# One block of a diffusion transformer on one core: ScalarE scales probabilities in two head pairs instead of four, and the five hand-written instruction lists and the bank table are dealt anew

## The chip, the cores and the metric

The kernel runs on one core of one Trainium2 chip. The metric is the device time in microseconds (us) of one launch. The kernel before takes 1402.81 us (median of 3 runs, 1401.66 to 1405.39). PE is TensorE, PEld its weight loads, DVE is VectorE, ACT ScalarE, POOL GpSimd and SP the engine that issues the loads and stores.

## The reference

32 batch elements, each 256 tokens of 128 features, go through one block: adaptive layer norm, causal attention with 16 heads of 64, and a feed-forward part that adds a gated MLP to a product-key expert lookup. Everything is float32.

```
h = layernorm(x) * (1 + ca) + sa
x = x + ga * attn(h)     # rmsnorm(h); q, k, v; softmax(q k^T * 64^-0.5, causal) v; sigmoid gates per head; Wout
h = layernorm(x) * (1 + cb) + sb
x = x + gb * ffn(h)
# ffn: silu(h Wg + bg) * (h Wu + bu) Wd + bd
#    + experts: sim = (h Wq) . keys, top 8 of 64 on both halves, their 8 best sums of 512,
#      softmax weights * silu(h . down_embed) into up_embed
```

## The kernel before, in words

One batch element is one turn (`body(i)`) of a software pipeline. Turn i runs the attention of batch i, the end of attention and the start of the FFN of batch i - 1, and the rest of the FFN of batch i - 2. Turns -1 and 0 have short lists of their own, turns 1 to 31 use the general list (3 to 30 of them in a hardware loop), and turn 32 has an own list again, which drains the pipeline. The change touches the general list, and two steps of turn 0.

Each engine has its own list of steps, written by hand: the calls at the end of `body` for POOL, ACT, DVE and PE. An engine works through its list strictly in that order, and each step begins with the semaphore waits it needs. So the order of the work is set by these lists alone; there is no planner.

The steps of attention go by pair of heads p = 0 to 7. On PE, `project_qk(p)` and `project_v(n)` (float32 split in a high and a low part, three matmuls each: the helper `mm3`, L1580 to L1582), then `scores(p)` (L1634, L1638), which works on halves of 64 rows of the array, `transpose_scores(p)` (L1648) and `weigh_values(p)` (L1661, L1665), which works on halves of 64 columns. All other work of PE uses the whole array of 128 x 128. Between them DVE takes the row maxima in place in PSUM (`row_max`, L1126), ACT the exponentials (`exp_scores`, L693), DVE the inverse and the coefficient (`invert` L1133, `coefficients` L1141) and the scaled probabilities (`normalise`, L1151). In the pairs listed in `SHARED`, DVE scales only head 0, and ACT scales head 1 with two activations (`scale_head`, L700). ACT copies the transposes to SBUF (`copy_transposes`, L685) and the outputs of `weigh_values` (L673).

Pairs take turns in two halves of the PSUM tensor pS. All other products of PE go through four PSUM banks, pW0 to pW3. The table `order` lists the 36 products of a turn; the n-th takes bank n mod 4, and has to wait until the product that stands before it in that bank is released by the engine that read it last. Thus the table decides who waits for whom: `("sim", 0)` is the first similarity product, `("hT", 0)` the transposed rows of the second layer norm, `("GU", c)` gate and up of the FFN, `("D", k)` the down products, `("ET", k)` the transposed expert weights, `("y", 0)` the FFN output.

Three chains matter below. `transpose_h` on PE writes hT; ACT modulates it (`modulate_h`, L793), makes its high part (`high_part`, L801), and DVE the low part (`low_part`, L1180), which releases it; only then can `similarity(0)` start. `gate_product(c)` (L1174) on DVE releases GU c. `shift(k)` (L1234) on DVE releases similarity k.

Of the kernel before, what the change touches and what calls it, by code (L numbers as in the profile page):

```python
# [43 lines left out]
SHARED = (1, 3, 5, 7)  # L44
# [3 lines left out]
def program(nc, x, norm_w, Wq, Wkv, Wout, Wgate, fWg, fbg, fWu, fbu, fWd, fbd, fWq, keys,  # L48
            down, up, cond, wmod, out):
    ctx = ExitStack()  # L50
    with ctx:
# [150 lines left out]
        def S(name):  # L202
# [33 lines left out]
        order = [("GU", 1, -2), ("D", 0, -2), ("V", 0, 0), ("PV", 6, -1), ("PV", 7, -1), ("V", 3, 0), ("QK", 2, 0),  # L236
# [232 lines left out]
        def _(pool):  # L469
# [24 lines left out]
            def body(i):  # L494
# [123 lines left out]
                candidates()  # L618
                products(1)
                rstd1()  # L620
                add_bias()
                weigh(0)
                add_heads(0)
                fold(0)
                rstd2()
                rms1()
                weigh(1)
                add_heads(1)
                fold(1)
# [4 lines left out]
        def _(act):  # L634
# [32 lines left out]
            def body(i):  # L667
# [150 lines left out]
                if isinstance(i, int) and i == 0:  # L818
# [16 lines left out]
                    scale_head(3)  # L835
# [22 lines left out]
                    scale_head(7)  # L858
# [48 lines left out]
                gate_up(1)  # L907
                down_tanh(0)
                copy_transposes(7, -1)
                values(0)  # L910
                exp_scores(0)
                weighted(6)
                values(3)
                weighted(7)
                queries(2)
                values(4)
                exp_scores(1)
                queries(3)
                queries(4)
                down_tanh(1)  # L920
                scale_head(1)
                copy_transposes(0, 0)
                copy_transposes(1, 0)
                queries(5)
                values(5)
                gate_up(2)
                exp_scores(2)
                exp_scores(3)
                total(0)
                values(1)  # L930
                gate_up(3)
                scale_head(3)
                queries(6)
                copy_transposes(2, 0)
                weighted(0)
                rows2()
                copy_transposes(3, 0)
                weighted(1)
                exp_scores(4)
                modulate_h()  # L940
                weighted(2)
                high_part(h2T_high, h2T, "hT")
                weighted(3)
# [7 lines left out]
                rms_scale()  # L951
                weighted(4)
                expert_exp(0)
                total(1)
                weighted(5)
                exp_scores(6)
                expert_exp(1)
                high_part(xT_high, xT, "xT")
                experts(1)
                exp_scores(7)  # L960
                scale_head(7)
                gate_up(0)
                copy_transposes(6, 0)
                queries(0)
                queries(1)
# [17 lines left out]
        def _(dve):  # L983
# [130 lines left out]
            def body(i):  # L1114
# [351 lines left out]
                bias_product(1)  # L1466
                ln1(aggregate1)
                gate_product(1)
                sum_top()
                gated_down(0)  # L1470
                row_max(0)
                invert_top()
                row_max(1)
                ln1(center1)
                choose(0, 0)
                choose(0, 1)
                invert(0)
                ln1(scale1)
                coefficients(0)
                invert(1)  # L1480
                normalise(0)
                coefficients(1)
                normalise(1)
                ln1(shift1)
                gated_down(1)
                choose(1, 0)
                row_max(2)
                row_max(3)
                invert(2)
                coefficients(2)  # L1490
                normalise(2)
                bias_product(2)
                invert(3)
                gate_product(2)
                gate_attention()
                add_residual()
                coefficients(3)
                stats2()
                aggregate2()
                ln1(square1)  # L1500
                normalise(3)
                bias_product(3)
                gate_product(3)
                choose(1, 1)
                row_max(4)
                row_max(5)
                invert(4)
                low_part(h2T_high, h2T, "hT")
                coefficients(4)
                normalise(4)  # L1510
                invert(5)
# [3 lines left out]
                row_largest(1)  # L1515
                shift(0)
                row_max(6)
                shift(1)
                invert(6)
                coefficients(6)  # L1520
                row_max(7)
                normalise(6)
                invert(7)
                coefficients(7)
                low_part(xT_high, xT, "xT")
                gate_output()
                finish()
                bias_product(0)
                gate_product(0)
                normalise(7)  # L1530
# [6 lines left out]
        def _(pe):  # L1537
# [49 lines left out]
            def body(i):  # L1587
# [268 lines left out]
                if isinstance(i, int) and i == B:  # L1856
# [55 lines left out]
                    late_project_up(1)  # L1912
                    return


                gate_up(1)
                project_down(0)
                transpose_scores(7, -1)
                project_v(0)
# [4 lines left out]
                project_v(3)  # L1924
                project_qk(2)
                project_v(4)
                project_qk(3)
                project_qk(4)
# [67 lines left out]
```

How the kernel before makes its waits and increments, by code:

```python
            def wait_free(self, name, k=0, after=(), off=None):  # L312
                job = self.apart(name, k, self.batch(name, k))
                if job:
                    for pn, pk in after:
                        self.wait_released(pn, pk, self.i + off)
                    full, free, n, count_n = job
                    if count_n > 1:
                        self.eng.wait_ge(free, count_n - 1)
                    elif (name, k, self.batch(name, k)) in drained:
                        pn, pk, turn = [j for m, j in enumerate(order) if m % NW == n and j[2] <= 0][-1]
                        self.wait_released(pn, pk, B - 1 + turn)
                    return
                need = {}
                prev = self.before(name, k)
                if prev and isinstance(self.i, int) and (prev[0], prev[1], self.i + prev[2]) in opened:
                    n = bank_of[name, k]
                    self.eng.wait_ge(open_free[n], n_opened[n])
                    if n == 0:
                        self.eng.wait_ge(su_act, 5)
                    prev = None
                for pn, pk, turn in [(*j, off) for j in after] + ([prev] if prev else []):
                    key = self.key(pn, pk)
                    need[key] = max(need.get(key, (turn, 0)), (turn, place[pn, pk] + 1))
                for key, (turn, n) in need.items():
                    self.eng.wait_ge(S(work_free[key]), self.nth(key, self.i + turn, n))
```

## Time and profile before

| | |
|---|---|
| median of 3 runs | 1402.81 us (1401.66 to 1405.39) |
| the profiled execution, its own time | 1400.69 us |
| its span, first to last instruction | 1398.8 us |
| PE busy / PEld busy | 1369.1 us (98%) / 1157.3 us (83%) |
| ACT / DVE / POOL busy | 1264.6 (90%) / 1214.9 (87%) / 1080.4 us (77%) |
| share of the chain that ended last | PE 93%, DVE 3%, ACT 2% |
| granted TensorE clock | 1.000 (2.4 GHz) |
| DMA | 27.74 MB, mean 20 GB/s |

The chain that ended last is followed back from the last instruction; 93% of it lies on PE. A turn of the loop is one period of a pattern that repeats 31 times. The ends of matmuls are modelled by the profiler, their starts are recorded: the difference of two starts is the reading to trust on PE. In the rows below, x4 on `scores` stands for two matmuls in two records each.

### The profile page before, as it was taken

How to read it: one execution, taken by the hardware profiler on the slowest of the kernel's cores; microseconds unless marked ns; L12 is line 12 of the kernel's file. 1: busy time of each engine (PE TensorE's matmuls, PEld its weight loads, DVE VectorE, ACT ScalarE, POOL GpSimd, SP SyncE). 2: the span in 40 equal slices, each digit the busy share in tenths (PEclk: the TensorE clock that was granted, in tenths of full speed). 3: DMA queues.
4: the chain of work that ended last, by engine and by line, in shares of the span. 5: the costliest groups of instructions: out<-in, count | busy, mean ns of one | idle time of the engine just before them, and what ended most of it. 6: DMA issues, size and time to landing. Idle time of an engine off the chain costs nothing.

```text
span 1398.8 us, 39734 instructions
## 1 busy us (share of the span) xinstructions
PE 1369.1 (98%) x11491; PEld 1157.3 (83%) x11491; DVE 1214.9 (87%) x5314; ACT 1264.6 (90%) x4212; POOL 1080.4 (77%) x1252
## 2 busy tenths in 40 slices
PE   6899999999999999999999999999999999999998
PEld 4778888888888888888888888888888888888877
DVE  6688898988898988898988898988898988898877
ACT  6889999999999999999999999999999999999975
POOL 2158888888888888888888888888888888888770
DMA  4000000000000000000000000000000000000000
GB/s 137 16 19 19 17 10 20 21 21 17 15 9 21 21 21 17 15 9 21 21 21 17 15 9 21 21 21 17 15 9 21 21 21 17 15 9 24 11 15 11
DMA packets 51042, 27.74 MB, mean 20 GB/s; under 512 B 10337, under 2 KB 50209, under 8 KB 51009
## 3 DMA queue, kind: packets, MB, share of 16 engines
q1 hardware_dynamic: 50768, 26.91, 7.3%
q10 hardware_dynamic: 240, 0.43, 0.1%
q8 instruction: 16, 0.26, 0.1%
q14 instruction: 18, 0.14, 0.0%
HBM read 23.02 MB, written 4.31 MB: 20 GB/s over the span
## 4 chain that ended last, share of the span: by engine, by line
PE 93%; DVE 3%; ACT 2%; issue 1%; POOL 1%; DMA 0%; SPq 0%; DVEq 0%; POOLq 0%
PE pW L1580 12%; PE pS L1648 12%; PE pW L1582 10%; PE pW L1581 10%; PE pW L1661 9%; PE pW L1689 8%; PE pS L1638 8%; PE pS L1634 7%; PE pW L1731 4%; PE pW L1734 4%; PE pW L1665 4%; PE pW L1722 2%; PE pW L1594 2%; ACT pS L693 1%; DVE pS L1126 0%
## 5 line engine op out<-in xcount | busy, mean ns | idle before, releaser
L693 ACT ACTIVATE pS<-pS,nmx 128x128 f32<-128x128 f32 (+1 forms) x1024 | 390.0, 437 | 31.3 <-DVE nmx L1126 30.7
L525 POOL TENSOR_TENSOR fexp<-fexp,fsum 128x512 f32<-128x512 f32 x240 | 316.5, 1347 | 90.6 <-DVE fexp L1277 90.6
L1126 DVE CUSTOM_DVE_ANT_0 pS<-pS,mask 128x128 f32<-128x128 f32 (+1 forms) x1024 | 332.3, 387 | 51.4 <-PE pS L1638 49.4
L516 POOL TENSOR_TENSOR fsum<-ex 128x512 f32<-128x512 f32 x248 | 251.8, 1047 | 1.3 <-ACT ex L741 1.3
L685 ACT COPY pT<-pS 128x768 f32<-128x768 f32 x256 | 206.1, 817 | 24.1 <-PE pS L1648 23.8
L1648 PE MATMUL pS<-ident,p_sb 128*128 128x128 f32 x1536 | 206.7, 274 | 6.8 <-DVE p_sb L1151 6.6
L1151 DVE TENSOR_TENSOR p_sb<-pS,coef 128x256 f32<-128x256 f32 (+2 forms) x512 | 208.9, 449 | 4.5
L693 ACT ACTIVATION_READ_ACCUMULATOR pS<-pS,nmx 128x1 f32 x1024 | 198.4, 194 | 0.0
L1648 PEld LDWEIGHTS pS<-ident,p_sb 128*128 128x128 f32 x1536 | 175.2, 141 | 27.6 <-DVE p_sb L1151 8.5
L1661 PE MATMUL pW<-pT,v 128*64 128x256 f32 x1024 | 162.3, 395 | 0.1
L1277 DVE TENSOR_SCALAR fexp<-fsum,top,rz 128x512 f32<-128x512 f32 x240 | 156.3, 702 | 0.0
L532 POOL TENSOR_TENSOR fexp<-fexp 128x512 f32<-128x512 f32 x120 | 152.4, 1291 | 4.7
L673 ACT COPY qk<-pW 128x512 f32<-128x512 f32 x256 | 154.6, 644 | 0.8 <-PE pW L1582 0.6
L1638 PE MATMUL pS<-qk 64*128 64x256 f32 x1024 | 155.1, 377 | 0.0
L1580 PE MATMUL pW<-xT_high,s_qkv_high 128*128 128x256 f32 x512 | 152.9, 299 | 1.3 <-DVE xT_low L1180 1.2
L1581 PE MATMUL pW<-xT_low,s_qkv_high 128*128 128x256 f32 x512 | 144.2, 282 | 0.0
L1582 PE MATMUL pW<-xT_high,s_qkv_low 128*128 128x256 f32 x512 | 143.9, 281 | 0.0
L1126 DVE DVE_READ_ACCUMULATOR2_ANT nmx<- 128x1 f32 x1024 | 141.5, 138 | 0.0
L1634 PE MATMUL pS<-qk 64*128 64x128 f32 x1024 | 120.7, 311 | 5.2 <-ACT pT L685 5.2
L1689 PEld LDWEIGHTS pW<-w_out,aoT 128*128 128x128 f32 x1024 | 116.8, 192 | 10.4 <-issue 10.3
L1689 PE MATMUL pW<-w_out,aoT 128*128 128x128 f32 x1024 | 122.7, 278 | 0.0
L1133 DVE RECIPROCAL pS<-pS 128x4 f32<-128x4 f32 x256 | 49.0, 192 | 82.3 <-ACT pS L693 82.2
(211 smaller groups left out, 3674.0 us busy)
## 6 DMA issues: line engine op xcount, KB each, us to landing
x_in<-in_L_attn_tokens SPq DMA_DIRECT2D x32, 128.0 KB, 2.1
x_res<-in_L_attn_tokens SPq DMA_DIRECT2D x32, 128.0 KB, 2.8
modB<-mods_dram SPq DMA_DIRECT2D x32, 128.0 KB, 2.9
modA<-mods_dram SPq DMA_DIRECT2D x31, 128.0 KB, 3.1
out<-yo SPq DMA_DIRECT2D x31, 128.0 KB, 1.9
modC<-mods_dram SPq DMA_DIRECT2D x32, 64.0 KB, 3.1
fsum<-in_L_attn_Wkv SPq DMA_DIRECT2D x1, 512.0 KB, 6.4
w_out<-in_L_attn_Wout SPq DMA_DIRECT2D x1, 512.0 KB, 7.3
```

The costliest lines, as they stand in the source:

```text
L516: ins = nc.gpsimd.tensor_tensor(fsum[:, k, h], ex[:, k, h, 0:NX].unsqueeze(2).broadcast_to([P, NX, NK]), ex[:, k, RH + h, :].unsqueeze(1). ...
L525: ins = nc.gpsimd.tensor_tensor(fexp[:, k, h, :], fexp[:, k, h, :], fsum[:, k, h].rearrange("p i j -> p (i j)"), ALU.mult)
L693: ins = nc.scalar.activation(ps, ps, ACT.Exp, bias=nmx[:, p % 2, h, k:k + 1], scale=-1.0, accum_out=den(p)[:, h, k:k + 1])
L1126: ins = nc.vector.tensor_tensor_reduce(out=ps, in0=ps, in1=mask[:, (1 - k) * P:2 * P], scale=-1.0, scalar=LARGEST, op0=ALU.add, op1=ALU.mi ...
L1580: mm(o, lhs[0], rhs[0], start=True, stop=False)
L1581: mm(o, lhs[0], rhs[1], start=False, stop=False)
L1582: return mm(o, lhs[1], rhs[0], start=False, stop=True)
L1634: mm(ps[:, h, 0:P], qk[r, p % 4, 0:P], qk[r, p % 4, N:N + P], start=True, stop=True, skip_group_check=True)
L1638: ins = mm(ps[:, h, P:SW], qk[r, p % 4, P:N], qk[r, p % 4, N:2 * N], start=False, stop=True, skip_group_check=True)
L1648: ins = tp(pS[:, p % 2, h, b * P:(b + 1) * P], p_sb[:, p % 2, h, b * P:(b + 1) * P], ident[:, :])
L1661: mm(bank[h * DH:(h + 1) * DH, 0:N], v[:, 0, hd], pT[:, p % 2, h, 0:2 * P], start=True, stop=False, skip_group_check=True)
L1689: ins = mm(w.bank("op")[:, k * D:(k + 1) * D], aoT[:, p, k * P:(k + 1) * P], w_out[:, p, :], start=p == 0, stop=p == NP - 1)
```

## The change

`SHARED` goes from pairs 1, 3, 5 and 7 to pairs 1 and 5: in pairs 3 and 7 DVE scales both heads, and the two `scale_head` steps of ACT go, in turn 0 too. The table `order` and the general lists of all four engines are written in another order. No other arithmetic is changed. The semaphore p1_ready counts two steps a turn instead of four.

```
-SHARED = (1, 3, 5, 7)
+SHARED = (1, 5)
...
-        order = [("GU", 1, -2), ("D", 0, -2), ("V", 0, 0), ("PV", 6, -1), ("PV", 7, -1), ("V", 3, 0), ("QK", 2, 0),
...
+        order = [("V", 3, 0), ("V", 0, 0), ("PV", 6, -1), ("PV", 7, -1), ("QK", 2, 0), ("V", 1, 0), ("QK", 3, 0),
+                 ("GU", 1, -2), ("GU", 2, -2), ("D", 0, -2), ("V", 4, 0), ("op", 0, -1), ("V", 5, 0), ("QK", 4, 0),
+                 ("PV", 0, 0), ("PV", 1, 0), ("D", 1, -2), ("QK", 5, 0), ("GU", 3, -2), ("PV", 2, 0), ("PV", 3, 0),
+                 ("hT", 0, -1), ("QK", 6, 0), ("QK", 7, 0), ("V", 2, 0), ("sim", 0, -1), ("ET", 0, -2),
+                 ("sim", 1, -1), ("PV", 4, 0), ("PV", 5, 0), ("y", 0, -2), ("ET", 1, -2), ("xT", 0, 1), ("QK", 0, 1),
+                 ("GU", 0, -1), ("QK", 1, 1)]
```

The general list of PE, new, with the old places of the steps left out:

```
+ transpose_scores(7, -1)  project_v(3)  project_v(0)  scores(0)  scores(1)  weigh_values(6)  weigh_values(7)
+ project_qk(2)  project_v(1)  project_qk(3)  gate_up(1)  transpose_scores(0, 0)  gate_up(2)  project_down(0)
+ transpose_scores(1, 0)  project_v(4)  scores(2)  scores(3)  project_out()  project_v(5)  project_qk(4)
+ weigh_values(0)  weigh_values(1)  project_down(1)  project_qk(5)  transpose_scores(2, 0)
+ transpose_scores(3, 0)  gate_up(3)  scores(4)  scores(5)  weigh_values(2)  weigh_values(3)  transpose_h()
+ project_qk(6)  project_qk(7)  project_v(2)  similarity(0)  transpose_experts(0)  transpose_scores(4, 0)
+ similarity(1)  transpose_scores(5, 0)  scores(6)  weigh_values(4)  weigh_values(5)  scores(7)
+ project_ffn(0)  transpose_experts(1)  transpose_x()  project_ffn(1)  transpose_scores(6, 0)  project_qk(0)
+ gate_up(0)  project_qk(1)
```

PE, the middle of a turn, before, from the transposes of pair 3 to `weigh_values` of pair 3 (pS<-qk is `scores`, pW<-pT,v is `weigh_values`, h is hT):

```order
L1648 MATMUL pS<-ident,p_sb 128x128 x6
L1634 MATMUL pS<-qk 128x128 x2
L1638 MATMUL pS<-qk 128x256 x2
L1661 MATMUL pW<-pT,v 64x256 x2
L1665 MATMUL pW<-pT,v 64x128 x2
L337 REGISTER_ALU
L1594 MATMUL pW<-ident,h 128x128 x2
L1634 MATMUL pS<-qk 128x128 x2
L1638 MATMUL pS<-qk 128x256 x2
L337 REGISTER_ALU
L1661 MATMUL pW<-pT,v 64x256 x2
L1665 MATMUL pW<-pT,v 64x128 x2
```

The same place now, with line numbers of the changed file:

```order
L1630 MATMUL pS<-qk 128x128 x2
L1634 MATMUL pS<-qk 128x256 x2
L364 REGISTER_ALU
L1630 MATMUL pS<-qk 128x128 x2
L1634 MATMUL pS<-qk 128x256 x2
L1657 MATMUL pW<-pT,v 64x256 x2
L1661 MATMUL pW<-pT,v 64x128 x2
L1657 MATMUL pW<-pT,v 64x256 x2
L1661 MATMUL pW<-pT,v 64x128 x2
L1590 MATMUL pW<-ident,h 128x128 x2
```

Scores 4 and 5 stand together, then `weigh_values` 2 and 3, and hT comes behind all four instead of between them.

DVE around the low part of hT, before: the maxima of pair 5, the inverse of pair 4, the low part, the coefficient and the probabilities of pair 4:

```order
L1126 ISA pS,nmx<-pS,mask 128x128
L1126 ISA nmx 128x1
L1126 ISA pS,nmx<-pS,mask 128x256
L1126 ISA nmx 128x1
L1133 RECIPROCAL pS<-pS 128x2x2
L1180 TENSOR_TENSOR h2T_low<-pW,h2T_high 128x256
L1141 SCALAR_TENSOR_TENSOR coef<-g_th,pS 128x4
L1151 TENSOR_TENSOR p_sb<-pS,coef 128x2x128
```

DVE there now, from the FFN products behind the maxima of pair 4 on (the four L1122 rows of `pS` are the maxima of pair 5):

```order
L1163 SCALAR_TENSOR_TENSOR pW<-pW,b_g,u_sb 128x256
L1170 SCALAR_TENSOR_TENSOR g_t<-g_t,pW 128x256
L1129 RECIPROCAL pS<-pS 128x2x2
L1137 SCALAR_TENSOR_TENSOR coef<-g_th,pS 128x4
L1117 REGISTER_ALU
L1122 ISA pS,nmx<-pS,mask 128x128
L1122 ISA nmx 128x1
L1122 ISA pS,nmx<-pS,mask 128x256
L1122 ISA nmx 128x1
L1122 ISA pS,nmx<-pS,mask 128x128
L1122 ISA nmx 128x1
L1122 ISA pS,nmx<-pS,mask 128x256
```

The inverse and the coefficient of pair 4 moved ahead of the maxima of pair 5; the low part of hT stands right behind those maxima as before, but now these follow the inverse.

## Rows read from the trace of the kernel before

**Rows 1.** The page, its first line.

```profile
span 1398.8 us, 39734 instructions
```

**Rows 2.** Chain in order of time: start, length, what; output projection of two bodies.

```profile
609.87 3.77 PE pW L1689 x32
...
651.83 3.77 PE pW L1689 x32
```

**Rows 3.** Busy us (x instructions): PE, PEld, DVE, ACT, POOL; clock; DMA share; GB/s.

```profile
426.00:468.00 42.00, 42.00 (x356) 35.62 (x355) 37.31 (x165) 38.95 (x131) 35.05 (x41) 1.00 0.06 17
```

**Rows 4.** Timeline of PE: start, length (us), instruction; scores 2, 3, output projection.

```profile
608.29 0.49 PE L1634 MATMUL pS<-qk 64*128 64x128 f32 x4
608.61 0.60 PE L1638 MATMUL pS<-qk 64*128 64x256 f32 x4
609.05 0.39 PE L1634 MATMUL pS<-qk 64*128 64x128 f32 x4
609.27 0.60 PE L1638 MATMUL pS<-qk 64*128 64x256 f32 x4
609.80 3.84 PE L1689 MATMUL pW<-w_out,aoT 128*128 128x128 f32 x32
```

**Rows 5.** Timeline of PE, where `project_v(1)` ends and gate/up 3 begins.

```profile
614.07 0.28 PE L1582 MATMUL pW<-xT_high,s_qkv_low 128*128 128x256 f32 x1
614.35 0.38 PE L1580 MATMUL pW<-h2T_high,s_g_high 128*128 128x256 f32 x1
614.57 0.28 PE L1581 MATMUL pW<-h2T_low,s_g_high 128*128 128x256 f32 x1
614.69 0.28 PE L1582 MATMUL pW<-h2T_high,s_g_low 128*128 128x256 f32 x1
```

**Rows 6.** Timeline of DVE: three instructions that free a bank.

```profile
613.88 0.42 DVE L1174 SCALAR_TENSOR_TENSOR g_t<-g_t,pW 128x256 f32<-128x256 f32 x1
...
622.65 0.42 DVE L1180 TENSOR_TENSOR h2T_low<-pW,h2T_high 128x256 fp32r<-128x256 f32 x1
...
629.27 0.68 DVE L1234 TENSOR_TENSOR sh<-pW,top_s 128x512 f32<-128x512 f32 x1
```

**Rows 7.** Timeline of PE, FFN output: first half, then second half.

```profile
630.01 1.15 PE L1731 MATMUL pW<-w_d,g_t 128*128 128x128 f32 x8
631.00 1.06 PE L1734 MATMUL pW<-w_up,eT 128*128 128x128 f32 x8
...
633.04 1.05 PE L1731 MATMUL pW<-w_d,g_t 128*128 128x128 f32 x8
633.93 1.06 PE L1734 MATMUL pW<-w_up,eT 128*128 128x128 f32 x8
```

**Rows 8.** Timeline of PE: scores 4, and the first transposes of the experts.

```profile
618.17 0.49 PE L1634 MATMUL pS<-qk 64*128 64x128 f32 x4
...
622.67 0.60 PE L1722 MATMUL pW<-ident,d_t 128*128 128x128 f32 x4
```

**Rows 9.** Timeline of DVE: row maxima of pair 4; pair 6 inverted, maxima of 7.

```profile
619.25 0.30 DVE L1126 CUSTOM_DVE_ANT_0 pS<-pS,mask 128x128 f32<-128x128 f32 x1 [0.48 <-PE pS L1638]
...
631.63 0.19 DVE L1133 RECIPROCAL pS<-pS 128x4 f32<-128x4 f32 x1 [1.68 <-ACT pS L693]
...
632.06 0.30 DVE L1126 CUSTOM_DVE_ANT_0 pS<-pS,mask 128x128 f32<-128x128 f32 x1
...
633.29 1.01 DVE L1151 TENSOR_TENSOR p_sb<-pS,coef 128x256 f32<-128x256 f32 x2
```

**Rows 10.** Timeline of ACT: first and last record of the exponentials of pair 4.

```profile
620.02 0.34 ACT L693 ACTIVATE pS<-pS,nmx 128x128 f32<-128x128 f32 x1
...
621.40 0.19 ACT L693 ACTIVATION_READ_ACCUMULATOR pS<-pS,nmx 128x1 f32 x1
```

**Rows 11.** Groups by shape, 400 to 1240 us: probabilities scaled by DVE.

```profile
L1151 DVE TENSOR_TENSOR p_sb<-pS,coef 128x512 f32<-128x512 f32 x80 | 54.3, 678 | 0.0
...
L1151 DVE TENSOR_TENSOR p_sb<-pS,coef 128x128 f32<-128x128 f32 x80 | 23.0, 287 | 1.4
```

More of the change, by code:

```diff
@@ L834, in body @@
                     queries(4)
-                    scale_head(3)
                     copy_transposes(2, 0)
@@ L1465, in body @@
                 ln1(stats1)
-                bias_product(1)
+                row_max(0)
+                row_max(1)
+                invert(0)
+                sum_top()
+                coefficients(0)
                 ln1(aggregate1)
[L1468 to L1471, printed above, removed]
+                normalise(0)
                 invert_top()
-                row_max(1)
                 ln1(center1)
+                invert(1)
+                coefficients(1)
+                normalise(1)
                 choose(0, 0)
                 choose(0, 1)
-                invert(0)
+                bias_product(1)
+                gate_product(1)
                 ln1(scale1)
[L1479 to L1486, printed above, removed]
                 row_max(2)
+                bias_product(2)
+                gate_product(2)
                 row_max(3)
+                gated_down(0)
+                gate_attention()
                 invert(2)
+                add_residual()
                 coefficients(2)
-                normalise(2)
-                bias_product(2)
                 invert(3)
-                gate_product(2)
-                gate_attention()
-                add_residual()
                 coefficients(3)
                 stats2()
+                normalise(2)
                 aggregate2()
-                ln1(square1)
                 normalise(3)
+                choose(1, 0)
+                choose(1, 1)
+                gated_down(1)
+                row_max(4)
                 bias_product(3)
                 gate_product(3)
-                choose(1, 1)
-                row_max(4)
+                invert(4)
+                coefficients(4)
                 row_max(5)
-                invert(4)
                 low_part(h2T_high, h2T, "hT")
-                coefficients(4)
                 normalise(4)
+                ln1(shift1)
                 invert(5)
@@ L1913, in body @@
                     return
-                gate_up(1)
-                project_down(0)
                 transpose_scores(7, -1)
+                project_v(3)
                 project_v(0)
@@ L1923, in body @@
                 weigh_values(7)
[L1924 removed]
                 project_qk(2)
[L1926 to L1935 removed]
+                project_v(1)
+                project_qk(3)
+                gate_up(1)
+                transpose_scores(0, 0)
+                gate_up(2)
+                project_down(0)
+                transpose_scores(1, 0)
+                project_v(4)
                 scores(2)
@@ L1938, in body @@
                 project_out()
-                project_qk(6)
-                gate_up(3)
-                transpose_scores(2, 0)
+                project_v(5)
+                project_qk(4)
                 weigh_values(0)
                 weigh_values(1)
+                project_down(1)
+                project_qk(5)
+                transpose_scores(2, 0)
                 transpose_scores(3, 0)
+                gate_up(3)
                 scores(4)
+                scores(5)
                 weigh_values(2)
+                weigh_values(3)
                 transpose_h()
-                scores(5)
-                weigh_values(3)
+                project_qk(6)
                 project_qk(7)
-                transpose_experts(0)
                 project_v(2)
                 similarity(0)
+                transpose_experts(0)
                 transpose_scores(4, 0)
@@ L1967, in body @@
                 project_qk(0)
+                gate_up(0)
                 project_qk(1)
```

80 lines of the change are left out of this document (35 added, 45 removed), and 5 rows, old and new, of the table order.

## The prediction, written before the changed kernel had run

> **What bounds the kernel now.** I read four views, in this order. The page first: the span is 1398.8 us [rows 1], and the profiled execution took 1400.69 us, 1.9 us around the span and 2.1 us under the median of 1402.81. The chain of waits in order of time second: it lies on PE, and the output projection of one turn starts at 609.87, that of the next at 651.83 [rows 2]. So a turn lasts 41.96 us, and the general list is run 31 times: 1301 of the 1399 us. Third the windows: in 42.00 us of the loop PE is busy for 42.00, DVE for 37.31, ACT for 38.95, POOL for 35.05, at the full clock [rows 3]. Nobody else is full. Last the timeline of PE, read by starts, since a full PE can still lose time in two ways that "busy" hides: by changing the shape in which it works, and by short waits that the modelled ends of matmuls cover. Both are there.
>
> Changes of shape. Scores work on halves of 64 rows, `weigh_values` (PV below) on halves of 64 columns, all else on the whole array; V n is `project_v(n)`. Two scores that follow each other start 609.05 - 608.61 = 0.44 apart (second part of the first to first part of the next), and a score and the output projection behind it 609.80 - 609.27 = 0.53: 0.09 for leaving the shape. The first scores after other work need 608.61 - 608.29 = 0.32 for their first part, the second 609.27 - 609.05 = 0.22: another 0.10 in the new shape [rows 4]. A change thus costs up to 0.19 us, and at least the 0.09 of leaving.
>
> Short waits. At 614.07 the last matmul of V 1 starts, at 614.35 the first of gate/up 3, at 614.57 its second, at 614.69 its third [rows 5]. The usual step is 0.12, so that the two steps of 0.50 hold 0.26 of waiting: the bank is released by gate_product, which ends at 613.88 + 0.42 = 614.30, 0.05 before PE starts [rows 6]. The same pattern stands three times more in a turn, each behind DVE. The FFN output starts at 630.01, 0.06 behind the end of shift(1) (629.27 + 0.68) [rows 6, 7]; its first half takes 631.00 - 630.01 = 0.99 to the next line, the second half, which waits for nobody, 633.93 - 633.04 = 0.89 [rows 7]: 0.10 lost. The low part of hT (622.65 + 0.42) ends just so before V 2, and the low part of xT before QK 0. I take 0.12 for each of these two, near the 0.10. In all 0.26 + 0.10 + 2 x 0.12 = 0.60 us a turn.
>
> The Trainium skill, "TensorEngine Tiling (Array Packing)", section Key Properties, says that changing the tiling mode drains TensorE, while changing the tile alone does not. Read so, a change between rows and columns would cost as much as one from the whole array, and the sum would be 3 x 0.19 instead of the 0.45 below. The rows here bear the direction out.
>
> **The change part by part.**
>
> Changes of shape go. Before, hT stood between two small groups: whole, scores 4, PV 2, hT, scores 5, PV 3, whole: six changes. Now it is whole, scores 4 and 5, PV 2 and 3, hT: three. In the rest of the list I count eleven before and eleven now (scores 0,1 and PV 6,7: three; scores 2,3: two; PV 0,1: two; scores 6, PV 4,5, scores 7: four). So 17 become 14. Three times 0.09 to 0.19 is 0.27 to 0.57; I take 0.15 each, nearer the scores rows, where both parts were seen: -0.45 us a turn.
>
> The four short waits go. In the new table gate/up 3 has PV 0 before it in its bank, which ACT copies out; V 2 has PV 3; the FFN output has the transposed experts; shift(1) and gate_product are no longer awaited there. QK 0 still needs the low part of xT, now 2.7 us behind xT (second half of the FFN output, transposes of pair 6), but DVE has it directly behind pair 6's probabilities. -0.60 us a turn; each may leave a rest, so 0.40 to 0.60.
>
> A new short wait comes. Similarity 0 needs the low part of hT, and DVE has put the inverse, the coefficient and the maxima of pair 5 in a row ahead of it. From the start of scores 4 the chain is: 1.08 to the first maxima (619.25 - 618.17) [rows 8, 9]; 0.77 to ACT's first exponential (620.02 - 619.25); 1.57 to the end of the last (621.40 + 0.19) [rows 10], and 0.03 to DVE; 0.43 from an inverse through the coefficient to the next maxima (632.06 - 631.63); 1.23 for these (633.29 - 632.06) [rows 9]; 0.42 for the low part, 0.06 to PE [rows 6, 7]. Sum 5.59 us. PE's way to similarity 0 in the same stretch: before, scores 4 to the first transposed experts took 622.67 - 618.17 = 4.50 [rows 8] and held scores 4 and 5, PV 2 and 3, hT and QK 7. Now QK 6 joins (6 steps of 0.12 = 0.71) and V 2 (3 steps of 384 columns, 0.18 each by their width, = 0.53); three shape changes leave, here at nearly their full price, 0.55: 5.19 us. PE arrives 0.40 early and waits: +0.40. From below, 0.2 if ACT and DVE hand over earlier than in these rows (the maxima may begin as soon as the scores end); from above 0.7, because the transposes of pair 5, scores 6 and PV 4 and 5 stand close behind on the same chain, and may each add a tenth.
>
> DVE and ACT. In pairs 3 and 7 DVE now scales both heads. Its shapes are 678 ns for 128x512 in place of 287 ns for 128x128, the 128x256 being in both [rows 11]: +0.39 us, twice a turn. DVE goes to 38.1 us of a turn of 41.3, and is still not full. ACT loses two pairs of activations. In the loop both are hidden by PE's list: transposes of pair 7 now have pair 6's transposes, QK 0, gate/up 0 and QK 1 before them, 2.8 us behind the FFN output, where DVE needs its 0.42 + 0.42 + 0.43 and 1.0 for pair 7, some 2.3. If that cover is gone, each tenth costs 3 us. In turn 0 there is little PE work to hide behind, and pairs 3 and 7 come 0.4 us later each: +0.8 us, between 0 and 2.
>
> The moved steps of POOL (bias, inverse roots, folds) cost nothing: POOL has 7 us free in 42, and its weighing of the experts is needed half a turn later. The loads on SP wait for the same releases and have turns to spare at 17 GB/s [rows 3]. Bounds for both: 0 to 2 us in all.
>
> Sum: 31 x (-0.45 - 0.60 + 0.40) = -20.2, and +0.8: -19.4 us. On the profiled execution 1400.69 - 19.4 = 1381.3; on the median shown 1402.81 - 19.4 = **1383 us**. Own range: -0.85 to -0.42 a turn, 1377 to 1391.
>
> **The rivals.**
>
> A: no new wait. The maxima of pair 5 run early enough and similarity 0 finds its operand. For it: DVE idled for 0.48 us before the maxima at 619.25 [rows 9], so it has room. Against it: the idle time ends in a wait for PE, the chain above is latency, and room does not shorten it. 31 x 1.05 = 32.6, less 0.8: 1371 us.
>
> B: no change. A PE that is busy 42.00 of 42.00 has nothing to give, the pipeline evens out the steps of 0.1 us. Against it the release times of rows 6, which stand right ahead of the late starts. 1403 us, within 3. The Trainium skill, "Perfetto Trace Analysis", section Identifying the Most-Contended Engine, warns that matmul busy is no measure of closeness to the limit and names the share of weight loads; that is 35.62 of 42.00 here, which speaks against this rival too.
>
> C: slower, through pair 7. Its probabilities are now wholly on DVE and stand behind gate_output and finish, which wait for the FFN output; its transposes open the next turn of PE. The slack worked out above is 0.5 us. It decides the sign once DVE is 0.5 + 0.65 = 1.15 us later than its rows say, for instance if the inverse of pair 7 finds ACT late with its exponentials. At 1.6 us late: 31 x 0.45 = +14, and 0.8: 1418 us. Against it: the idle times of DVE, 1.68 us before one inverse alone [rows 9].
>
> D: half the gain. The wait of similarity 0 is 0.7 and the followers on its chain take another tenth or two: 31 x 0.2 = 6, less 0.8: 1398 down to 1391 us.
>
> **How the numbers follow.** Forecast 0.63, A 0.15, D 0.13, B 0.05, C 0.04. The range is 1371 to 1395: it takes in A and most of D. About 0.3% (4 us) is what a measurement of this kernel tells from no change. Faster holds the forecast, A and most of D: 0.90; within 0.3% B and a rest of D: 0.06; slower 0.04.
>
> **What would show it.** The chain in order of time should have output projections about 41.3 us apart. In the PE timeline scores 5 should start 0.76 behind scores 4, gate/up 3 and V 2 should step by 0.12 and 0.18 from their predecessors, and the first similarity matmul should start 0.06 behind the end of L1176 on DVE, with some 0.4 us more than a step before it. A turn of 40.9 would show rival A, one of 41.96 rival B; a wait of the transposes of pair 7 for p_sb in the loop would show C. My sum would be wrong if the price of a shape change is paid again somewhere else, or if a wait that I have not placed stands in the second half of the turn.

## The result: slower, against the prediction

The changed kernel takes 1416.57 us (median of 3, 1415.22 to 1417.55) against 1402.81 before: ratio 1.0076, 95% interval 1.0056 to 1.0096, so 0.8% slower. Predicted was 1383. The profiled execution took 1417.55 us, its span is 1415.8.

### The profile page after: what moved, and what is told of

The parts are those of the page before. It is cut to its first block, busy times and chain, and to the rows that moved or that the text cites. A ratio compares the mean times of both kernels' runs of the same rounds, so it can differ in the third digit from the quotient of the medians.

```text
span 1415.8 us, 40018 instructions
## 1 busy us (share of the span) xinstructions
PE 1366.0 (96%) x11491; PEld 1161.4 (82%) x11491; DVE 1253.4 (89%) x5314; ACT 1230.7 (87%) x4084; POOL 1069.6 (76%) x1252
## 4 chain that ended last, share of the span: by engine, by line
PE 39%; POOL 20%; DVE 15%; issue 14%; ACT 11%; DMA 0%; ACTq 0%; SPq 0%; POOLq 0%; DVEq 0%
POOL fexp L525 10%; PE pS L1644 6%; POOL fexp L532 5%; DVE pS L1122 5%; PE pS L1634 4%; PE pW L1727 4%; PE pW L1730 4%; ACT pS L693 4%; PE pS L1630 4%; PE pW L1576 3%; PE pW L1657 3%; PE pW L1577 3%; PE pW L1578 3%; POOL wsum L535 3%; DVE h L1031 2%
## 5 line engine op out<-in xcount | busy, mean ns | idle before, releaser
L693 ACT ACTIVATE pS<-pS,nmx 128x128 f32<-128x128 f32 (+1 forms) x1024 | 397.1, 456 | 59.0 <-DVE nmx L1122 58.8
L525 POOL TENSOR_TENSOR fexp<-fexp,fsum 128x512 f32<-128x512 f32 x240 | 304.1, 1299 | 107.1 <-DVE fexp L1273 107.1
L1122 DVE CUSTOM_DVE_ANT_0 pS<-pS,mask 128x128 f32<-128x128 f32 (+1 forms) x1024 | 333.0, 390 | 56.6 <-PE pS L1634 55.2
L1147 DVE TENSOR_TENSOR p_sb<-pS,coef 128x256 f32<-128x256 f32 (+2 forms) x512 | 233.4, 498 | 4.6
L693 ACT ACTIVATION_READ_ACCUMULATOR pS<-pS,nmx 128x1 f32 x1024 | 216.7, 212 | 0.0
L673 ACT COPY qk<-pW 128x512 f32<-128x512 f32 x256 | 172.7, 675 | 16.2 <-PE pW L1578 15.9
L532 POOL TENSOR_TENSOR fexp<-fexp 128x512 f32<-128x512 f32 x120 | 156.7, 1326 | 4.7
L1122 DVE DVE_READ_ACCUMULATOR2_ANT nmx<- 128x1 f32 x1024 | 144.8, 141 | 0.0
L1630 PEld LDWEIGHTS pS<-qk 64*128 64x128 f32 x1024 | 82.8, 185 | 43.7 <-issue 25.9
L1273 DVE TENSOR_SCALAR fexp<-fsum,top,rz 128x512 f32<-128x512 f32 x240 | 115.0, 544 | 0.0
```

The source lines that it names most:

```text
L525: ins = nc.gpsimd.tensor_tensor(fexp[:, k, h, :], fexp[:, k, h, :], fsum[:, k, h].rearrange("p i j -> p (i j)"), ALU.mult)
L532: ins = nc.gpsimd.tensor_tensor(fexp[:, k, h, :], fexp[:, k, h, :], fexp[:, k, h + 1, :], ALU.add)
L693: ins = nc.scalar.activation(ps, ps, ACT.Exp, bias=nmx[:, p % 2, h, k:k + 1], scale=-1.0, accum_out=den(p)[:, h, k:k + 1])
L1122: ins = nc.vector.tensor_tensor_reduce(out=ps, in0=ps, in1=mask[:, (1 - k) * P:2 * P], scale=-1.0, scalar=LARGEST, op0=ALU.add, op1=ALU.mi ...
L1147: ins = nc.vector.tensor_tensor(o, pS[:, p % 2, mine, cols_of(k)], coef[:, p % 2, mine, k:k + 1].broadcast_to(o.shape), ALU.mult)
L1630: mm(ps[:, h, 0:P], qk[r, p % 4, 0:P], qk[r, p % 4, N:N + P], start=True, stop=True, skip_group_check=True)
```

## The profile after

The page of the changed kernel: the span answers to [rows 1], the second line is the busy time of each engine, the last the shares of the chain that ended last ("issue" is time in which an engine waited for nothing that the profile shows).

```profile
span 1415.8 us, 40018 instructions
...
PE 1366.0 (96%) x11491; PEld 1161.4 (82%) x11491; DVE 1253.4 (89%) x5314; ACT 1230.7 (87%) x4084; POOL 1069.6 (76%) x1252
...
PE 39%; POOL 20%; DVE 15%; issue 14%; ACT 11%; DMA 0%; ACTq 0%; SPq 0%; POOLq 0%; DVEq 0%
```

PE is still busy for 96%, but it is no longer the chain: 39%, where [rows 2] lay on PE from turn to turn. The window of one turn, with the columns of [rows 3]:

```profile
594.00:636.30 42.30, 41.74 (x356) 35.58 (x354) 38.50 (x165) 37.88 (x127) 34.52 (x40) 1.00 0.06 17
```

PE now leaves half a microsecond of a turn open, and DVE has gone from 37.31 to 38.50 us.

Where the 17.0 us between the two spans stand is read from the first scores of a turn. I counted from turn 3 to turn 31, 28 turns, and what lies ahead and behind (starts on PE in us; the last column is the span less the second):

| kernel | scores 0 of turn 3 | of turn 31 | mean turn | behind it |
|---|---|---|---|---|
| before | 135.75 | 1311.37 | 41.99 | 87.43 |
| changed | 138.50 | 1325.95 | 42.41 | 89.82 |

The loop lost 11.8 us, the start 2.75, the end 2.4. The forecast was a turn of 41.31.

In the loop both executions ran at a granted clock of 1.00. Outside it they did not: in the changed kernel's execution the clock fell to its lower level, 1.2 GHz, for 3.4 us three times, at 33.7, 91.7 and 1368.3 us, and in that of before never. The same stretch in both (columns as above), changed kernel first:

```profile
33.70:37.10 3.40, 3.40 (x18) 2.65 (x14) 1.37 (x8) 0.80 (x1) 0.00 (x0) 0.50 0.00 0
```

```profile
33.70:37.10 3.40, 3.40 (x34) 2.62 (x34) 1.37 (x8) 1.89 (x6) 0.00 (x0) 1.00 0.00 0
```

PE issued 18 matmuls in place of 34. From 20 to 30 us it had been busy for 7.74 us, before for 7.72, so its own work doesn't tell the two executions apart. Part of what the start and the end lost is therefore the clock and not the change.

The steps on PE can be checked one by one. Timeline of PE in the changed kernel, start and length in us (scores 4 and 5; end of V 2 and similarity 0; end of similarity 1 and transposes of pair 5; first half of the FFN output):

```profile
625.91 0.49 PE L1630 MATMUL pS<-qk 64*128 64x128 f32 x4
...
626.65 0.46 PE L1630 MATMUL pS<-qk 64*128 64x128 f32 x4
...
631.08 0.34 PE L1578 MATMUL pW<-s_qkv_high,xT_low 128*128 128x384 f32 x1
631.68 0.47 PE L1576 MATMUL pW<-s_sim_high,h2T_high 128*128 128x512 f32 x1 [0.27 <-DVE h2T_low L1176]
...
634.03 0.39 PE L1578 MATMUL pW<-s_sim_high,h2T_low 128*128 128x512 f32 x1
634.71 0.87 PE L1644 MATMUL pS<-ident,p_sb 128*128 128x128 f32 x6 [0.29 <-ACT p_sb L700]
...
638.80 1.16 PE L1727 MATMUL pW<-w_d,g_t 128*128 128x128 f32 x8
639.80 1.06 PE L1730 MATMUL pW<-w_up,eT 128*128 128x128 f32 x8
```

Scores 5 stand 0.74 behind scores 4 (0.76 predicted). Similarity 0 starts 0.60 behind the last matmul of V 2, whose step is 0.18: a wait of 0.42, predicted 0.40. The transposes of pair 5 were predicted to follow their predecessor; a step of similarity is 0.23, here it is 0.68: a wait of 0.45, in other turns up to 0.77 (0.58 in the mean), that no step of mine had. It is behind DVE, by way of ScalarE, which scales head 1 of pair 5. The chain of the same turn in order of time (start, length, what):

```profile
631.26 0.28 DVE h2T_low L1176
631.54 0.93 DVE p_sb L1147 x2
632.47 1.12 DVE h L1031
...
633.73 0.17 DVE coef L1137
...
634.19 0.48 ACT p_sb L700
...
634.71 0.87 PE pS L1644 x6
```

`ln1(shift1)` (h <- h, modA) now stands between the probabilities of pair 4 and the inverse of pair 5, and takes 1.12 us of the chain. Groups by shape from 400 to 1240 us, before and after: count, busy us, mean ns.

```profile
L1277 DVE TENSOR_SCALAR fexp<-fsum,top,rz 128x512 f32<-128x512 f32 x160 | 104.5, 704 | 0.0
L1035 DVE TENSOR_TENSOR h<-h,modA 128x256 f32<-128x256 f32 x20 | 10.6, 532 | 0.0
L1041 DVE CUSTOM_DVE_ANT_0 sq<-h 128x128 f32<-128x128 f32 x40 | 10.1, 289 | 0.0
L1026 DVE TENSOR_TENSOR h<-h,modA 128x256 f32<-128x256 f32 x20 | 8.1, 404 | 0.0
```

```profile
L1273 DVE TENSOR_SCALAR fexp<-fsum,top,rz 128x512 f32<-128x512 f32 x160 | 76.7, 544 | 0.0
L1031 DVE TENSOR_TENSOR h<-h,modA 128x256 f32<-128x256 f32 x20 | 26.1, 1305 | 0.0
L1037 DVE CUSTOM_DVE_ANT_0 sq<-h 128x128 f32<-128x128 f32 x40 | 18.4, 494 | 0.0
L1022 DVE TENSOR_TENSOR h<-h,modA 128x256 f32<-128x256 f32 x20 | 17.2, 859 | 0.0
```

The same four operations on the same data: shift1 went from 532 to 1305 ns, scale1 from 404 to 859, square1 from 289 to 494, and `choose` down from 704 to 544. The operations with an input in PSUM kept their lengths within 0.02 us. What changed for these four is what POOL does meanwhile. Timeline of DVE and of POOL in the changed kernel, two turns:

```profile
632.38 1.21 DVE L1031 TENSOR_TENSOR h<-h,modA 128x256 f32<-128x256 f32 x1
...
674.69 1.51 DVE L1031 TENSOR_TENSOR h<-h,modA 128x256 f32<-128x256 f32 x1
```

```profile
632.04 1.28 POOL L532 TENSOR_TENSOR fexp<-fexp 128x512 f32<-128x512 f32 x1
...
674.65 1.27 POOL L532 TENSOR_TENSOR fexp<-fexp 128x512 f32<-128x512 f32 x1
```

POOL's instruction ends at 632.04 + 1.28 = 633.32, shift1 at 632.38 + 1.21 = 633.59. In the other turn POOL ends at 675.92, shift1 at 676.20. Shift1 ends 0.27 or 0.28 behind the end of the POOL instruction in flight, whenever it started. It isn't slowed, it is held. The trace of before, which I had, says so already (DVE, then POOL):

```profile
606.20 0.55 DVE L1035 TENSOR_TENSOR h<-h,modA 128x256 f32<-128x256 f32 x1
...
607.27 2.32 DVE L1277 TENSOR_SCALAR fexp<-fsum,top,rz 128x512 f32<-128x512 f32 x2
```

```profile
605.17 1.29 POOL L525 TENSOR_TENSOR fexp<-fexp,fsum 128x512 f32<-128x512 f32 x1
...
607.86 1.45 POOL L525 TENSOR_TENSOR fexp<-fexp,fsum 128x512 f32<-128x512 f32 x1
```

POOL ends at 606.46, shift1 at 606.75; it had started so late in POOL's instruction that it lost a tenth. The two `choose` end at 607.27 + 2.32 = 609.59, which is 0.28 behind POOL's 609.31. Elsewhere a `choose` takes 0.54.

The Trainium skill, "SBUF — State Buffer", section Who interferes with whom, states this: VectorE and GpSimd share one pair of ports as an exclusive lock; a VectorE instruction with two SBUF inputs contends with a GpSimd instruction that reads SBUF, so does one in a 2-port mode, and "Whoever issues first gets the shared pair for the whole instruction". The trace agrees: two inputs (shift1, scale1, square1) are held and so is `choose` with one, those with an input in PSUM aren't, and POOL's instructions that start behind a held one read 1.45 to 1.47 us in place of 1.28. No row here shows in which mode `choose` runs. The prediction didn't weigh this rule.

## Experiments

Three theories. **L, lock**: three operations of layer norm 1 (scale1, shift1, square1) were moved to places where POOL's long instructions run, and the wait stands on the way to the transposes of pair 5. **P, POOL's path**: masks, weighing, weighted sum, `total(0)` early in ScalarE's list, then ScalarE and DVE, bound the turn whatever shift1 does. **D**: DVE has too much to do since it scales pairs 3 and 7. All ratios are to the kernel before, and a turn is the mean of the 28.

**x1_shift_moved.** One move in the changed kernel:

```
                 choose(1, 1)
+                ln1(shift1)
                 gated_down(1)
...
                 normalise(4)
-                ln1(shift1)
                 invert(5)
```

> The changed kernel with one move: shift1 (h <- h, modA) stands behind choose(1, 1), where POOL runs its short instructions, and no longer between the probabilities and the inverse of pair 5. Theory L (lock): a DVE operation that reads two operands from SBUF, or the mask comparison, and that starts while a 512-column TENSOR_TENSOR of POOL runs, ends only 0.28 us behind the end of that instruction. Then shift1 falls from 1.2 or 1.5 us to about 0.42, the coefficient of pair 5 comes 1.2 us earlier and the transposes of pair 5 no longer wait; but square1, still beside POOL, and shift(0) behind it keep the bank that weigh_values(5) needs, so the turn falls only from 42.45 to something between 41.9 and 42.45: 1400 to 1417 us. Theory P (POOL and ACT's path from the masks through the weighted sum to total(0) bounds the turn): shift1 plays no part, 1416. Theory D (DVE has too much work since it scales pairs 3 and 7): shift1's length stays with its place changed, and the time stays at 1416.

Measured 1394.51 us, ratio 0.9914 (0.9887 to 0.994): 22 us under the changed kernel by one moved instruction, and faster than before. The turn is 41.54. Trace of x1, one line of the kernel (times min/median/max in ns):

```profile
L1031 DVE TENSOR_TENSOR h<-h,modA x20: 411/416/419, 409.9 to 1199.0; 128x256 f32<-128x256 f32 x20
```

And PE, from similarity 1 to the transposes of pair 5: the step is 0.23, the wait is gone.

```profile
626.49 0.40 PE L1578 MATMUL pW<-s_sim_high,h2T_low 128*128 128x512 f32 x1
626.72 0.49 PE L1644 MATMUL pS<-ident,p_sb 128*128 128x128 f32 x3
```

Summed over the same places of PE's list, turn by turn, the changed kernel's mean turn is 0.87 us longer than that of x1: 0.63 at the transposes of pair 5, 0.12 at `weigh_values(5)`, the rest in pieces of 0.02 to 0.06. I had expected at most 0.5, since I took square1 to stay at 0.7. It fell to 0.28, because it now starts 0.13 before the end of POOL's instruction; that gave the turn more than I had allowed. P and D expected no change from this move, and fall as the cause of these 22 us.

**x2_shift_square.** x1, and square1 goes behind `shift(0)`:

```
                 row_largest(0)
-                ln1(square1)
                 shift(0)
+                ln1(square1)
```

> As the first, and square1 stands behind shift(0) instead of ahead of it. Theory L: both operations that waited for POOL are off the path from similarity 0 to weigh_values(4) and (5); the turn falls to about 42.0, 1398 to 1405 us. Theories P and D: no change from the changed kernel, 1414 to 1418.

1395.38 us, ratio 0.9934 (0.9911 to 0.9957), turn 41.57. Faster than expected, but no better than x1: the first half of square1 stands beside POOL again (0.92 us), now behind `shift(0)`.

**x12_square_moved** is the move of square1 alone.

> The changed kernel with square1 alone moved behind shift(0); shift1 stays where it meets POOL. Theory L: the transposes of pair 5 still wait their 0.6 us a turn for the coefficient behind shift1, only the 0.12 before weigh_values(5) goes: turn 42.25 to 42.4, 1410 to 1416. If it were DVE's amount of work around row_largest(0) that cost the time, this move would win as much as x2, 1395.

1416.60 us, ratio 1.0091 (1.0064 to 1.0118), turn 42.35, as L expects; shift1 takes 1.33 us in the mean. Of the two, shift1 carries the loss.

**x3_pairs_back.** `SHARED = (1, 3, 5, 7)`, and `scale_head(3)` and `scale_head(7)` back in ScalarE's list ahead of `copy_transposes(2, 0)` and `(6, 0)`.

> The changed kernel with pairs 3 and 7 shared again (ScalarE scales their first heads, as before), each at its old place ahead of the copies of the next transposes. Theory D: DVE gets 0.78 us a turn back and the time falls by 10 to 25 us, to 1392 to 1407. Theory P: ACT's list between total(0) and the exponentials of pair 5 grows by 0.48 us for the head of pair 3, and the turn with it, 1425 to 1450. Theory L: the lock's cost is untouched by DVE's share; the same 0.48 us on ACT stands on the chain to the coefficient of pair 5, so 1420 to 1450 also.

1474.44 us, ratio 1.05 (1.0465 to 1.0536), turn 44.26. DVE is down to 37.45 us a turn, and the kernel is 58 us slower than the changed one. Its ScalarE and PE (start, length, idle before):

```profile
602.28 0.64 ACT L768 ACTIVATE junk<-wsum 128x512 f32<-128x512 f32 x1 [0.56 <-POOL wsum L535]
...
603.86 0.74 ACT L700 ACTIVATE p_sb<-pS,coef 128x128 f32<-128x128 f32 x2
```

```profile
602.74 0.82 PE L1648 MATMUL pS<-ident,p_sb 128*128 128x128 f32 x6
604.66 0.55 PE L1648 MATMUL pS<-ident,p_sb 128*128 128x128 f32 x3 [1.10 <-ACT p_sb L700]
```

The head of pair 3 stands behind `total(0)`, which waits for POOL, and PE waits for it in each turn. From the turn of the changed kernel to this one PE is 1.32 us longer at that place, where I had put 0.48; the other 0.5 us stands mainly around scores 0 to 3 and wasn't traced further. So in this order ScalarE mustn't have pair 3. As this run adds a wait of its own, it doesn't refute D by itself; x1 does, where DVE has the same work as in the changed kernel and the loss is gone.

**x7_before_two_pairs**: the kernel before with that part of the change alone (no `scale_head` of 3 and 7).

> The kernel before with one part of the change alone: pairs 3 and 7 are scaled wholly by DVE, and ScalarE's two operations for them go. Every list keeps its order. Prediction's view (the cover holds in the loop): 1403 plus 1 to 3 for turn 0. Against it: in the order of before the transposes of pair 7 stand early in the turn and the probabilities of pair 7 are the last on DVE, so each tenth that they are later stands on PE: with 0.39 us behind ScalarE's 0.48 in parallel, up to 0.4 us a turn and 2.2 us in turn 0: 1405 to 1418.

1407.62 us, ratio 1.0018 (1.0007 to 1.0029), turn 42.11, above the 1404 to 1406 that the prediction's view gave: in the order of before the cover holds but for 0.12 us a turn, of which 0.09 stands ahead of the transposes of pair 3.

**x4_before_shift_later**: the kernel before, with two neighbours swapped.

```
-                ln1(shift1)
                 gated_down(1)
+                ln1(shift1)
                 choose(1, 0)
```

> The kernel before with two neighbours of DVE swapped: shift1 now stands behind gated_down(1) instead of ahead of it, so that it starts some 0.6 us later, when POOL is well inside its next TENSOR_TENSOR. Theory L: shift1 takes 1.3 to 1.6 us in place of 0.53, all behind it on DVE is 0.9 us later, and gate/up 3 and V 2 wait for DVE; the turn grows by 0.8 to 1.4 us: 1425 to 1445. If the lengths of DVE's operations don't depend on where in POOL's instruction they start, 1403 within 3.

1441.06 us, ratio 1.0256 (1.0226 to 1.0286), turn 43.25. DVE, POOL and PE of x4:

```profile
627.25 1.12 DVE L1035 TENSOR_TENSOR h<-h,modA 128x256 f32<-128x256 f32 x1
628.30 2.91 DVE L1277 TENSOR_SCALAR fexp<-fsum,top,rz 128x512 f32<-128x512 f32 x2
```

```profile
626.81 1.29 POOL L525 TENSOR_TENSOR fexp<-fexp,fsum 128x512 f32<-128x512 f32 x1
```

```profile
634.51 0.28 PE L1582 MATMUL pW<-xT_high,s_qkv_low 128*128 128x256 f32 x1
635.98 0.39 PE L1580 MATMUL pW<-h2T_high,s_g_high 128*128 128x256 f32 x1 [1.19 <-DVE g_t L1174]
```

626.81 + 1.29 = 628.10, shift1 ends at 628.37. No other kernel of this study is so plain: no instruction was added, none changed its engine, and the swap costs 1.26 us a turn, 1.23 of it at this one place.

**x5_halves**: the changed kernel with POOL's additions of heads cut in two.

```
-    ins = nc.gpsimd.tensor_tensor(fexp[:, k, h, :], fexp[:, k, h, :], fexp[:, k, h + 1, :], ALU.add)
+    for c in range(0, NE, NE // 2):
+        ins = nc.gpsimd.tensor_tensor(fexp[:, k, h, c:c + NE // 2], fexp[:, k, h, c:c + NE // 2],
+                                      fexp[:, k, h + 1, c:c + NE // 2], ALU.add)
```

> The changed kernel; only POOL's additions of two heads (L532) are cut into halves of 256 columns, so that four instructions of some 0.7 us stand where two of 1.3 stood. DVE's list is untouched. Theory L (a DVE operation on two SBUF operands waits for the end of the POOL instruction in flight): shift1 can wait for at most one short instruction, so it falls from 1.2 or 1.5 us to 0.4 to 0.95, although as much POOL work as before runs beside it; the turn falls by 0.2 to 0.9 us, 1390 to 1411. If DVE and POOL shared bandwidth instead, each slowed in proportion, shift1 would stay at 1.2 to 1.5 us and the time at 1416 or a little over.

1431.38 us, ratio 1.0191 (1.0169 to 1.0213): the length as L expects, the time as nobody did. DVE, POOL and PE of x5:

```profile
639.98 0.81 DVE L1033 TENSOR_TENSOR h<-h,modA 128x256 f32<-128x256 f32 x1
...
642.71 0.27 DVE L1039 CUSTOM_DVE_ANT_0 sq<-h 128x128 f32<-128x128 f32 x1
...
642.91 1.35 DVE L1039 CUSTOM_DVE_ANT_0 sq<-h 128x128 f32<-128x128 f32 x1
```

```profile
639.77 0.73 POOL L533 TENSOR_TENSOR fexp<-fexp 128x256 f32<-128x256 f32 x1
...
642.84 1.28 POOL L537 TENSOR_TENSOR wsum<-fexp 128x512 f32<-128x512 f32 x1
```

```profile
644.93 0.65 PE L1659 MATMUL pW<-pT,v 128*64 128x256 f32 x4 [0.50 <-DVE sh L1232]
```

Shift1 ends at 640.79, 0.29 behind the short instruction (640.50), so it waits for an instruction and doesn't share with it. A shared bandwidth, by which shift1 would have stayed at 1.2 to 1.5, is out. But all behind it is earlier by some tenths now, and the second square1 starts just behind the start of the weighted sum's 1.28 us: it takes 1.35, shift(0) is late, and `weigh_values(5)` waits for its bank. Place by place on PE, against the changed kernel: 0.51 us a turn less ahead of the transposes of pair 5, 0.60 more at `weigh_values(5)`, and 0.28 more ahead of scores 4, which wait for ScalarE's copy of the transposes. That copy stands behind `total(0)`, which needs POOL's weighted sum, and the four short instructions take longer than the two long ones; this link is argued, not tried. The lock was not removed, it caught the next operation.

**x6_experts_first** and **x8_total_later.** On x1: `("ET", 0, -2)` and `("sim", 0, -1)` change places in the table and in PE's list; then `total(0)` behind `down_tanh(1)` on ScalarE.

> The first experiment (shift1 behind choose(1, 1)) and one swap on PE and in the table of banks: the transposes of experts 0 stand ahead of similarity 0 instead of behind it. There PE waited 0.41 us a turn for the low part of hT (last matmul of V 2 at 623.56, first of similarity at 624.15). If that wait is only PE's, it is filled by 0.44 us of transposes and the turn falls from 41.53 to 41.1 or 41.2: 1380 to 1387. Theory P (the turn is a loop through the masks, POOL's weighing, total(0) on ACT and the low part): similarity 0 starts when it did, PE's work behind it is shorter by 0.44, and the loop is shorter too, so the gain is the same unless another link of that loop, such as the coefficient of pair 5, is next at once; then 1390 to 1395.

> As x6_experts_first, and total(0) stands behind down_tanh(1) in ScalarE's list, so that ScalarE doesn't wait 0.6 us for POOL's weighted sum. Theory P: ScalarE reaches the exponentials of pairs 4 and 5 some 0.4 us earlier and the turn falls by a further 0.1 to 0.4 us, 3 to 12 us under x6. If PE alone is the bound by then, the same as x6 within 3.

x6: 1392.70 us, ratio 0.9911 (0.989 to 0.9931), turn 41.50, 0.03 under x1. It missed the 1380 to 1387 expected and fell in P's 1390 to 1395: the transposes of experts 0 took over the place in the banks behind hT, and wait for the low part of hT to free it, just as similarity 0 did. x8: 1390.01 us, ratio 0.9896 (0.9875 to 0.9916), turn 41.40, the fastest kernel here. The shares of the chain that ended last on its page:

```profile
PE 77%; ACT 12%; DVE 6%; issue 4%; DMA 0%; SPq 0%; POOL 0%; DVEq 0%; ACTq 0%; POOLq 0%
```

POOL has 0% of it, where the changed kernel had 20% and x1 20% too. P's path was real, and worth 0.1 us a turn once shift1 was out of POOL's way.

**x9_one_more_shape**: x8 with `project_down(1)` between `weigh_values(0)` and `(1)`.

> As x8_total_later, but on PE and in the table of banks project_down(1) stands between weigh_values(0) and (1) instead of behind both, so that PE leaves and takes up the column shape once more in a turn. From the rows of x8 (first matmul of a weighing 0.48 to its second line against 0.43 in the shape, 0.21 in place of 0.12 for the last step before it, 0.33 in place of 0.23 for the first step behind it) the pair of changes costs 0.24 us, so 2 x 0.15 as the prediction took would be 0.30: the turn goes from 41.40 to 41.64 or 41.70, 1397 to 1400 us. If changes cost nothing once DVE and ACT pace PE, the time of x8, 1390 within 3.

1421.22 us, ratio 1.0125 (1.0103 to 1.0146), turn 42.43: 1.03 us where 0.24 to 0.30 was expected. At the place of the edit PE needs 0.80 + 0.89 + 0.80 + 0.81 for the two weighings, `project_down(1)` and the keys of pair 5, in x8 1.45 + 0.80 + 0.71 (sums of starts): 0.34, or 0.17 for each change of shape. The other 0.7 stands further on: 0.54 of it around the FFN output, whose second half waits for ScalarE's copy of the transposed expert weights; in ScalarE's list that copy stands behind the exponentials that need shift(1). On DVE, the lock is there again (DVE, POOL of x9):

```profile
638.58 1.31 DVE L1037 CUSTOM_DVE_ANT_0 sq<-h 128x128 f32<-128x128 f32 x1
```

```profile
638.47 1.27 POOL L535 TENSOR_TENSOR wsum<-fexp 128x512 f32<-128x512 f32 x1
```

In x8 square1 started 0.2 before the end of a POOL instruction, and its first half took 0.36 to 0.40. Here it starts 0.1 behind the start of the next, and takes 1.31, with both shifts behind it. That these 0.9 us are the 0.54 on PE fits the order of the lists; no run moved square1 away to show it.

**x10_scale_early** and **x11_search**: scale1 behind `choose(0, 1)`, shift1 behind `choose(1, 1)`, square1 behind `shift(0)`, with x6's swap and x8's `total(0)`; x11 moves three entries of ScalarE's list besides.

> All three operations away from POOL's long instructions: scale1 right behind choose(0, 1), where it starts before POOL's first weighing has (403 ns there in the kernel before, 0.86 us in the changed one), shift1 behind choose(1, 1), square1 behind shift(0); with the swap of x6 and the later total(0) of x8. Theory L: scale1 0.40 to 0.45, shift1 0.42, square1 below 0.9 and off the path; the turn is at most that of x8, 41.2 to 41.4: 1383 to 1390 us. Theory P expects the same as x8, since POOL's weighing starts no earlier (or 0.1 us later, behind scale1).

> As x10_scale_early with three small moves in ScalarE's list: gate_up(1) behind the copies of transposes 0, experts(0) ahead of the copies of transposes 4, exp_scores(6) ahead of weighted(4). Nobody's theory gives these a price above 0.1 us a turn: 1383 to 1390, within 3 of x10.

1393.65 us, ratio 0.9929 (0.9907 to 0.9952), turn 41.57; and 1396.86, ratio 0.995 (0.9933 to 0.9966), turn 41.62. Scale1 and shift1 take 0.42 us in both, as L says. Both times missed my 1383 to 1390: the first half of square1, beside the weighted sum, takes 1.0 us ahead of the maxima of pair 6. Of the 0.17 us a turn lost to x8, PE has 0.10 at the FFN output and 0.06 at gate/up 0. I hold this place of square1 for it, but it wasn't tried by itself, and x2, which has square1 there too and the same turn, loses to x8 at other places (0.07 at similarity 0). Of the 3 us between x11 and x10 the turn explains 1.5; which of the three entries costs them wasn't tried.

## Why the prediction was wrong, step by step

**Changes of shape, -0.45 a turn: right.** 0.15 each was taken, x9 gives 0.17. By the starts on PE the scores and weighings, 12.43 us a turn before, take 12.09 in x1: 0.34 of the 0.45. In x9 a pair of changes costs 0.34, of which 0.2 stands in the steps just ahead of and just behind the group, where some of the rest can be.

**Short waits, -0.60: two right, one right by luck, one wrong.** (The row at 614.07 in [rows 5], and the prediction's sentence on it, say V 1; by its operands and by PE's list it is QK 6. The wait is the same.) The projection of pair 6 (QK 6) and gate/up 3 behind it took 0.95 + 0.81 us before; two such groups in x1 that wait for nobody (QK 0, gate/up 0) take 0.79 + 0.70: 0.27 of waiting, 0.26 predicted. The transposes ahead of QK 0 had 0.14, and that is gone. V 2 is 0.10 shorter in its first step, 0.28 before and 0.17 now, but for the most part that was no wait: V 1 before (607.59 to 607.85) and V 4 in the changed kernel (613.59 to 613.85) need 0.26 for the same step, and all three stand behind transposes, as V 2 no longer does. The size was right, the cause wasn't.

The FFN output gave back 0.05 of its 0.10. From the second part of scores 7 to the second line of the first half, with the transposes of x, PE took 631.00 - 629.21 = 1.79 before and takes 1.52 + 0.22 = 1.74 now. Its first half, now right behind scores 7 and with nothing to wait for, still takes 639.80 - 638.80 = 1.00, the price of leaving the shape. Before, the transposes of x stood between the two, so whether the 0.10 in [rows 7] was a wait for shift(1) isn't shown.

**Similarity 0, +0.40: right**, 0.42, and by the mechanism named. From scores 4 the chain took 631.68 - 625.91 = 5.77 us where 5.59 was forecast, PE's way 5.35 for 5.19: each link was near its row, and the errors of 0.18 and 0.16 nearly cancel.

With these terms alone the turn would be 41.31, with 0.10 for the FFN output put back 41.41. x1 has 41.54 and x8 41.40.

**DVE and POOL, 0: the step that failed.** I wrote that both are "hidden by PE's list" and that the moved steps of POOL "cost nothing". I priced DVE by the two pairs alone, whose cover did hold (0.12 in x7, in the order of before), and gave the moved operations of layer norm 1 no price, because they were moved and not added. Their length depends on what POOL has in flight: 0.41 alone, up to 1.5 beside an instruction of 1.3. The cost is the 0.87 us between x1 and the changed kernel, and 28 x 0.87 = 24 us is more than the whole forecast gain. Of the 33.6 us between forecast and result this one instruction's place is 22 by x1's time; the rest is the 0.23 us that x1's turn has over the forecast, and the start and the end. The prediction named the right place, "the transposes of pair 5 ... stand close behind on the same chain, and may each add a tenth"; it was 0.63.

**Turn 0, +0.8: not found.** Start and end cost 2.75 + 2.4 = 5.1 us outside the 28 turns. Scores 5 of turn 0, the first place where the wholly scaled pair 3 can show, start at 36.61 before and at 37.99, 39.99, 38.38 and 36.34 in the changed kernel, x1, x2 and x8, which are the same program up to there. The scatter is the clock: x8 had no stretch at 0.50 ahead of that place, and is no later there than the kernel before; the changed kernel had one stretch at 0.50 ahead of it, x1 two (at 25.1 and 35.3), and in x2 PE stepped by 0.21 us in place of 0.12 up to 16.9 us. A stretch of 3.4 us at half the clock costs up to 1.7. So pair 3 shows no price at that place, and neither does pair 7: its transposes start at 52.85 before and at 52.60 in x8.

The end is 1.2 to 2.4 us longer in the kernels of the new order (88.6 to 89.9 behind scores 0 of turn 31; x3, with its own wait, has 91.5). The changed kernel, x1, x2, x6 and x10 had a stretch at 0.50 41 to 43 us behind those scores and lie at 89.8 to 89.9; x8, x5, x12, x9 and x11 had none there and lie at 88.6 to 89.0. So of the 2.4 us half goes with the clock. What of the other 1.2 is work that the new list puts later in a turn, and what is lost, stays open.

**The rivals.** C gave 1418, 1.4 off the result, by a mechanism that didn't happen: the transposes of pair 7 don't wait in the loop (0.57 us, as anywhere). A number that fits isn't a cause that fits. B (no change) said that a full PE has nothing to give: it gave 0.45 us a turn in x1 and 0.59 in x8.

## What to carry to other kernels

Before moving a VectorE instruction, look at its operands: if both lie in SBUF, or its length in the trace comes in clearly different sizes (540, 900 and 1490 ns for `choose` in the kernel before), its duration belongs to the place and not to the operation, and GpSimd's row beside it must be read at the old place and at the new one. Put such instructions where GpSimd runs short ones or waits, and never take a mean of them as a price. And where a kernel's time hangs on which side of an instruction's end another begins, an edit of 0.3 us elsewhere can cost 1 us: x9 and x5 were both thrown by it. Last, compare the granted clock stretch by stretch before reading anything into the first and last turns: a mean of 0.996 hid three stretches at 0.50.

## What was not expected of the hardware

- A held DVE instruction shows no idle time and no releaser in the trace. Its recorded length grows instead, up to 1.51 us from 0.41 (1.54 in x12), so no view of waits names it.
- The one behind pays little: POOL's instruction that follows a held one takes 1.46 us in place of 1.28, while DVE loses up to 1.1.
- Not every POOL instruction holds DVE. In x8 shift1 starts at 612.17, 0.19 us into a 0.65 us instruction of POOL on 128x2 elements, and takes 0.41. Up to what size this goes wasn't tried.
- A DVE instruction that starts between two of POOL gets its turn: scale1 beside the weighing took 0.40 where it began 0.07 us ahead of POOL, 0.86 where 0.7 us behind its start.
